# Distance attention: the 16-bit high halves of the probabilities made by ScalarE instead of VectorE

## The chip, the cores and the metric

One Trainium2 chip, one of its cores. The metric is the device time of one execution of the whole program in microseconds (us); lower is better. The engines run side by side and meet at semaphores: TensorE (PE, with its weight loads PEld), VectorE (DVE), ScalarE (ACT), GpSimd (POOL) and SyncE (SP), which only issues DMAs here.

## The reference, cut to what matters

The program is a stack of four residual layers on `x` of 2 x 2048 x 256 in float32. The third of them is the distance attention that the change touches; the second and the fourth are mixtures of experts.

```python
x = x + _L0_attn_a_ref(_layernorm(x))                 # head attention, causal
x = x + _L0_ffn_ref(_layernorm(x), Wr, W1, b1, W2, b2)
x = x + _L0_attn_b_ref(_layernorm(x), Wq, bq, Wk, bk, Wv, bv, Wo, bo)
x = x + _L0_ffn_ref(_layernorm(x), Wr, W1, b1, W2, b2)

# _L0_attn_b_ref
q, k, v = x @ Wq + bq, x @ Wk + bk, x @ Wv + bv
dist_sq = q_sq[:, :, None] + k_sq[:, None, :] - 2.0 * (q @ k.T)
scores = exp(-dist_sq)
attn = softmax(scores)
out = (attn @ v) @ Wo + bo
```

## The kernel before

**Precision.** TensorE is fed with 16-bit floats. To keep float32 accuracy each operand is split in a high half (the value rounded to 16 bits) and a low half (what the rounding lost), and `split_product` (L1042 to L1046) makes three matmuls of each product: high by high, high by low, low by high. So each tile of probabilities is needed twice, as `phi` and as `plo`, both scaled by `Scales.PROBS` = 4096.

**Steps.** `distance_attention` (from L1567) works on 8 chunks of 512 queries (4 for each of two sequences) and, in a chunk, 16 tiles of 128 keys: 128 steps n = 0 to 127. Each engine has a loop of its own over n. In step n:

- PE: `scores(n)`, 6 matmuls of 512 columns into one of two banks; it waits until `dist(n-2)` has been read. Then `weighted(n-4)`, 12 matmuls of 256 columns; it waits for `phi(n-4)` and `plo(n-4)`.
- DVE: `dist(n)` (L2055) reads the bank and adds the queries' lengths. Then `halves(n-2)`: `phi` (L1996, a multiplication that rounds to 16 bits) and `plo` (L1998, in float32 the difference to `phi`).
- ACT: `score(n)` (L1904), the inner exponential, waits for `dist(n)`. Then `second(n-1)` (L1874 to L1879), the exponential of the softmax, into `p32`, a ring of R = 3.
- POOL: `accumulate(n-1)` (L1938, L1941) adds up `p32` for the denominators.

`phi` and `plo` are rings of HR = 4; a slot is free again once `weighted` of four steps before has been done (`s_pv`).

**Work between the steps.** The order is written out by hand: the table `AT` names, for a step n, further tasks that each engine does behind its work of that step, in the order of the table. `norm` (DVE, L1015) and `turn` (PE transposes L1023, then ACT `high` L1028, then DVE `low` L1038) make the normalized columns of later queries and keys; `values` (PE, ACT L1860, DVE L1969) and `project` (PE, ACT L1869 and its square L1872, DVE L1979) make values, queries and keys. `lengths` (PE, L1782) needs the squares of a projection's two halves, which POOL has added up first (L1925). `turn` and `values` share one PSUM bank, `turns`, so each waits until ACT and DVE have read the one before. DVE reads a projection only when ACT has also squared it. Projections are at steps 0 to 11, 22, 23, 53 to 70, 86 and 87. Some of the table, for the steps that the prediction goes through:

```python
4: [("turn", 5), ("norm", 6)],
5: [("values", 3), ("lengths", 3), ("project", 4, 0), ("norm", 7)],
6: [("turn", 6), ("project", 4, 1)],
7: [("turn", 7), ("lengths", 4)],
51: [("turn", 10)],
52: [("turn", 11)],
53: [("project", 8, 0), ("norm", 12)],
54: [("values", 8), ("project", 8, 1), ("norm", 13)],
55: [("lengths", 8), ("project", 9, 0)],
58: [("values", 10), ("project", 10, 1), ("norm", 14)],
61: [("turn", 14), ("project", 12, 0), ("lengths", 11)],
62: [("values", 12), ("project", 12, 1)],
```

From step 89 on DVE also adds up the normalized rows for the router, one tile a step (`gathered`, L375 and L378). Steps 119 to 126 prepare the next mixture: `weights` (ACT L1113, DVE L1122), `gates`, and `scale_b2` (DVE L1199), for which PE's `widen_b2` (L1203) waits.

Of the kernel before, what the change touches and what calls it, by code (L numbers as in the profile page):

```python
# [35 lines left out]
ALU = mybir.AluOpType  # L36
ACT = mybir.ActivationFunctionType
# [18 lines left out]
class Program:  # L56
# [41 lines left out]
    def sb(self, ctx):  # L98
        return lambda name, shape, dt: ctx.enter_context(self.nc.sbuf_tensor(name, shape, dt))
# [1467 lines left out]
def distance_attention(pr, block, w, cols, mix, queries, banks_free, free_ahead):  # L1567
# [11 lines left out]
    with ExitStack() as ctx:  # L1579
        sb, ps = pr.sb(ctx), pr.ps(ctx)  # L1580
        QR, DR, R, HR = 3, 2, 3, 4
# [9 lines left out]
        p32 = sb("d_p32", [P, R, CHUNK], F32)  # L1591
        phi = sb("d_phi", [P, HR, CHUNK], F16)
# [84 lines left out]
        def turn_bank(kind, p):  # L1677

            return {("turn", 2): banks[:, 0, :], ("values", 0): banks[:, 1, :]}.get((kind, p), turns[:])

        def project_out(i, m):
            kind, g = tasks[i]
            if kind == "k":
                c = g % CHUNKS
                return khi[:, m, c * CHUNK:(c + 1) * CHUNK], klo[:, m, c * CHUNK:(c + 1) * CHUNK]
            return queries[:, g % QR, 0, m, :], queries[:, g % QR, 1, m, :]

        def square(i):
            return w.sums if i == 1 else w.squares

        def step(n):
            chunk, kt = divmod(n, TILES)
            return chunk, kt, chunk // CHUNKS, chunk % CHUNKS == 0

        def summed(n):

            return (TILES - 1) * (n // TILES) + max(n % TILES, 1)
# [25 lines left out]
        @block.sync  # L1723
        def _(sp):
            chosen = mix.chosen(sp, 0, routing)
            mix.load_biases(sp, 0, chosen)
            sp.wait_ge(s_len, len(tasks))
            mix.load_weights(sp, 0, chosen, range(len(mix.early_raw)))
# [123 lines left out]
        @block.scalar  # L1852
        def _(act):
            def high(p):
                cols.high(act, BASE + p, turn_bank("turn", p))

            def values_high(p):
                act.wait_ge(s_v, p + 1)
                t = 2 * (p % (TILES // 2))
                act.activation(vhi[:, t:t + 2, :], turn_bank("values", p).rearrange("p (t d) -> p t d", t=2), ACT.Copy,  # L1860
                               scale=Scales.VALUES)\
                   .then_inc(s_vhi, 1)

            def project_high(i, m):
                kind, g = tasks[i]
                j = KD * i + m
                bias = w.bias_s[:, 0 if kind == "q" else 1, m:m + 1]
                act.wait_ge(s_p, j + 1)
                act.activation(project_out(i, m)[0], outs[:, BANKS[i] + m, :], ACT.Identity, bias=bias).then_inc(s_hi, 1)  # L1869
                if i >= 2 and m == 0:  # L1870
                    act.wait_ge(s_len, 1 if i == 2 else i)
                act.activation(square(i)[:, m, :], outs[:, BANKS[i] + m, :], ACT.Square, bias=bias).then_inc(s_sq, 1)  # L1872

            def second(n):  # L1874
                act.wait_ge(s_score, n + 1)
                if n >= R:
                    act.wait_ge(s_plo, n - R + 1)
                    act.wait_ge(s_acc, summed(n - R))
                act.activation(p32[:, n % R, :], score[:, n % 2, :], ACT.Exp).then_inc(s_p32, 1)  # L1879

            def tanh():
                mix.tanh(act, 0, routing)

            def weights_high(i):
                act.wait_ge(s_qk, TILES * (NG - 2 + i // 2))
                mix.part_high(act, 0, i)

            do = {"turn": high, "values": values_high, "project": project_high, "tanh": tanh, "weights": weights_high}
            act.activation(rden[0:1, 0, 0:1], pr.ones[0:1, 0:1], ACT.Exp).then_inc(s_table, 1)
            project_high(0, 0)  # L1890
            project_high(0, 1)
            project_high(1, 0)
            project_high(1, 1)
            high(2)
            high(3)
            values_high(0)
            for n in range(STEPS):
                chunk, kt, b, first = step(n)
                act.wait_ge(s_dist, n + 1)
                if first and kt % TPC == 0:  # L1900
                    act.wait_ge(s_lenc, task["k", chunk + kt // TPC] + 1)
                if n >= 2:
                    act.wait_ge(s_p32, n - 1)
                act.activation(score[:, n % 2, :], dist[:, n % DR, :], ACT.Exp, scale=pr.scales.distance,  # L1904
                               bias=nksq[:, b, kt:kt + 1]).then_inc(s_score, 1)
                if n >= 1:
                    second(n - 1)
                for kind, *what in AT.get(n, ()):
                    if kind in do:
                        do[kind](*what)  # L1910
            second(STEPS - 1)

        @block.gpsimd
# [45 lines left out]
        def _(dve):  # L1959
# [30 lines left out]
                       .then_inc(s_lenc, 1)  # L1990

            def halves(n):
                dve.wait_ge(s_p32, n + 1)
                if n >= HR:
                    dve.wait_ge(s_pv, n - HR + 1)
                dve.tensor_scalar(phi[:, n % HR, :], p32[:, n % R, :], Scales.PROBS, None, ALU.mult).then_inc(s_phi, 1)  # L1996
                dve.wait_ge(s_phi, n + 1)
                dve.scalar_tensor_tensor(out=plo[:, n % HR, :], in0=p32[:, n % R, :], scalar=Scales.PROBS, in1=phi[:, n % HR, :],  # L1998
                                         op0=ALU.mult, op1=ALU.subtract)\
                   .then_inc(s_plo, 1)  # L2000
# [46 lines left out]
            for n in range(STEPS + 2):  # L2047
# [9 lines left out]
                if n >= 2:  # L2057
                    halves(n - 2)
# [102 lines left out]
```

## Time and profile before

| | us |
|---|---|
| median of 3 runs | 1654.05 (1653.84 to 1654.17) |
| profiled execution, device time | 1654.1 |
| its span (first to last instruction in the trace) | 1652.4 |
| distance attention, first `dist` to last `weighted` | about 877 to 1305 |

A row of the timeline gives the start in us from the span's start, the duration, the engine, the line of the kernel, the operation, output<-input by the program's names, its form, and in brackets how long the engine had been idle before it and what ended that. `distance_raw` is memory that the sums of the denominators and the squares share. Matmuls are pipelined: the next one starts before the modelled end of the one before, so for TensorE the starts are what counts.

### The profile page before, as it was taken

Reading aid. Unit: us, or ns where it says so; the run is one execution under the profiler, and the core shown is the slowest. Engines: PE = TensorE matmul, PEld = TensorE weight load, DVE = VectorE, ACT = ScalarE, POOL = GpSimd, SP = SyncE. Lnnn points to the kernel's source line nnn. Section 1 sums busy time; section 2 is a strip of 40 time slices with the busy share of each in tenths; the row PEclk is TensorE's granted clock in tenths of the full one; section 3 lists DMA queues with packets and bytes.
Section 4 is the critical chain, followed back from the end, with each engine's and each line's share of the span. In section 5 each row is a group of like instructions: output and inputs, shape, how many; then the busy total and the mean of one; then the engine's idle time right before and its main releaser. Section 6 shows DMA issues by size and latency. Waiting matters only on the chain.

```text
span 1652.4 us, 30850 instructions
## 1 busy us (share of the span) xinstructions
PE 1607.8 (97%) x11947; PEld 891.8 (54%) x11947; DVE 1069.2 (65%) x2159; ACT 987.2 (60%) x1260; POOL 358.9 (22%) x466
## 2 busy tenths in 40 slices
PE   6999999999999999999999999999999899999998
PEld 2222222222233666666675666666666566666666
DVE  7533454454335975785557688868898887576554
ACT  6999999999998433433336554555445443353332
POOL 3022122122021000000005445544444300000000
PEclk9999999999999999999999999999999999999999
DMA  4013235100030003000000000000000200300000
GB/s 135 20 28 115 77 116 166 23 15 17 20 110 1 1 1 103 1 1 1 1 1 1 1 1 2 1 1 2 1 1 27 77 1 1 128 13 14 13 13 26
DMA packets 44335, 52.92 MB, mean 32 GB/s; under 512 B 3664, under 2 KB 39071, under 8 KB 44191
## 3 DMA queue, kind: packets, MB, share of 16 engines
q1 hardware_dynamic: 44190, 50.96, 9.8%
q8 instruction: 96, 1.57, 0.4%
q14 instruction: 49, 0.39, 0.1%
HBM read 38.88 MB, written 4.19 MB: 26 GB/s over the span
## 4 chain that ended last, share of the span: by engine, by line
PE 66%; ACT 16%; issue 11%; DVE 6%; DMA 0%; POOL 0%; ACTq 0%; DVEq 0%; SPq 0%; POOLq 0%
ACT a_probs L781 15%; PE f_ypsum L1045 7%; PE f_ypsum L1046 7%; PE f_ypsum L1044 7%; PE f_h L1044 7%; PE f_h L1045 7%; PE f_h L1046 7%; PE a_out L539 4%; PE d_outs L1044 3%; PE d_outs L1046 3%; PE d_outs L1045 3%; PE d_banks L1044 2%; PE d_banks L1046 2%; PE d_banks L1045 2%; PE a_scores L919 2%
## 5 line engine op out<-in xcount | busy, mean ns | idle before, releaser
L781 ACT ACTIVATE a_probs<-a_scores 128x1024 f32<-128x1024 f32 x544 | 499.9, 1208 | 8.2 <-PE a_scores L919 8.1
L1395 ACT ACTIVATE f_gelu<-f_h,f_bcol,s_more 128x512 f32<-128x512 f32 x256 | 199.0, 778 | 398.0 <-PE f_h L1046 386.3
L539 PE MATMUL a_out<-a_probs,a_values 128*32 128x512 f32 (+3 forms) x2560 | 294.0, 540 | 6.6 <-ACT a_probs L781 5.6
L1450 DVE TENSOR_SCALAR f_hh<-f_gelu,f_gates_scaled 128x512 f16<-128x512 f32 x256 | 136.7, 534 | 196.7 <-ACT f_gelu L1395 195.8
L1904 ACT ACTIVATE d_score<-d_dist,d_nksq,s_more 128x512 f32<-128x512 f32 x128 | 104.1, 813 | 191.8 <-DVE d_dist L2055 190.0
L1045 PE MATMUL f_ypsum<-f_w,f_hh 128*128 128x256 f16 x768 | 209.3, 273 | 0.0
L1046 PE MATMUL f_ypsum<-f_w,f_hl 128*128 128x256 f16 x768 | 209.3, 273 | 0.0
L1044 PE MATMUL f_ypsum<-f_w,f_hh 128*128 128x256 f16 x768 | 209.3, 273 | 0.0
L1452 DVE SCALAR_TENSOR_TENSOR f_hl<-f_gelu,f_gates_scaled,f_hh 128x512 f16<-128x512 f32 x256 | 192.2, 751 | 9.1
L919 PE MATMUL a_scores<-a_moving,a_fixed 64*128 64x512 f16 (+3 forms) x1280 | 184.0, 354 | 9.6 <-ACT a_probs L781 3.7
L795 POOL TENSOR_SCALAR_AFFINE_SELECT a_probs<-a_probs 128x256 f32<-128x256 f32 (+1 forms) x224 | 98.6, 456 | 420.7 <-ACT a_probs L781 412.5
L1941 POOL TENSOR_TENSOR distance_raw<-distance_raw,d_p 128x512 f32<-128x512 f32 x112 | 146.3, 1306 | 178.4 <-ACT d_p L1879 178.2
L1469 POOL TENSOR_TENSOR x<-x,f_b_wide 128x256 f32<-128x256 f32 x64 | 52.9, 848 | 523.6 <-DVE c_xn L1015 523.5
L1044 PE MATMUL f_h<-c_xhi,f_w 128*128 128x512 f16 x384 | 145.6, 379 | 1.3 <-DVE f_w L1122 1.2
L1045 PE MATMUL f_h<-c_xlo,f_w 128*128 128x512 f16 x384 | 145.5, 379 | 0.0
L1046 PE MATMUL f_h<-c_xhi,f_w 128*128 128x512 f16 x384 | 145.5, 379 | 0.0
L919 PEld LDWEIGHTS a_scores<-a_moving,a_fixed 64*128 64x128 f16 x1280 | 49.0, 94 | 173.3 <-ACT a_probs L781 118.7
L1045 PE MATMUL d_outs<-d_vlo,d_phi 128*128 128x256 f16 x512 | 139.6, 273 | 0.0
L1046 PE MATMUL d_outs<-d_vhi,d_plo 128*128 128x256 f16 x512 | 139.6, 273 | 0.0
L1044 PE MATMUL d_outs<-d_vhi,d_phi 128*128 128x256 f16 x512 | 139.6, 273 | 0.0
L618 DVE COPY a_moving<-a_out 128x1024 f16<-128x1024 f16 x31 | 21.4, 692 | 141.5 <-PE a_out L867 141.4
L539 PEld LDWEIGHTS a_out<-a_probs,a_values 128*32 128x32 f32 x2560 | 55.5, 108 | 96.0 <-issue 71.6
(271 smaller groups left out, 2737.9 us busy)
## 6 DMA issues: line engine op xcount, KB each, us to landing
f_raw<-in_L_ffn_W SPq DMA_DIRECT2D x16, 1024.0 KB, 7.6
f_raw<-in_L_ffn_W SPq DMA_DIRECT2D x24, 512.0 KB, 8.8
a_fixed<-a_moving SPq DMA_DIRECT2D x60, 96.0 KB, 2.3
x<-in_L_attn_a_x SPq DMA_DIRECT2D x7, 512.0 KB, 6.0
out<-x SPq DMA_DIRECT2D x7, 512.0 KB, 2.9
f_raw<-in_L_ffn_W SPq DMA_DIRECT2D x12, 256.0 KB, 4.0
a_fixed<-a_moving SPq DMA_DIRECT2D x60, 32.0 KB, 2.0
f_early_raw<-in_L_ffn_W SPq DMA_DIRECT2D x4, 256.0 KB, 3.4
```

The source lines that it names most:

```text
L539: mm = pe.matmul(spare[32 * j:32 * j + 32, i % 2, skip:skip + w], values[:, G % 2, kt + tile, j, :], probs[:, u % UR, j % 2, col:col + w], ...
L781: act.activation(probs[:, u % UR], scores[:, 2 * (u % SR):2 * (u % SR) + 2, :], ACT.Exp, scale=HD ** -0.5)\
L795: pool.affine_select(out=tri, in_=tri, compare_op=ALU.is_ge, fill=0.0, base=0, pattern=[[0, tri.shape[1]], [1, P]], channel_multiplier=-1) ...
L919: mm = pe.matmul(scores[:, 2 * (u % SR) + h, col_of[a]:col_of[a] + w], fixed[G % 2][head, a, k0:k0 + P], moving[G % 2][head, a, q0:q0 + w] ...
L1044: pe.matmul(out, fixed_hi, moving_hi, start=first, stop=False, skip_group_check=shared)
L1045: pe.matmul(out, fixed_hi, moving_lo, start=False, stop=False, skip_group_check=shared)
L1046: return pe.matmul(out, fixed_lo, moving_hi, start=False, stop=last, skip_group_check=shared)
L1395: act.activation(gel[:, n % HR, :], hps[:, n % 2, :], ACT.Gelu, bias=mix.bcol[:, q, FT * e + j:FT * e + j + 1], scale=pr.scales.hidden)\
L1450: dve.tensor_scalar(hh[:, n % HR, :], gel[:, n % HR, :], gate, None, ALU.mult).then_inc(s_hh, 1)
L1452: dve.scalar_tensor_tensor(out=hl[:, n % HR, :], in0=gel[:, n % HR, :], scalar=gate, in1=hh[:, n % HR, :], op0=ALU.mult, op1=ALU.subtract) ...
L1904: act.activation(score[:, n % 2, :], dist[:, n % DR, :], ACT.Exp, scale=pr.scales.distance, bias=nksq[:, b, kt:kt + 1]).then_inc(s_score, 1)
L1941: pool.tensor_tensor(acc, acc, p32[:, n % R, :], ALU.add).then_inc(s_acc, 1)
```

## The change

ScalarE makes `phi` itself, right behind the exponential whose result it reads: a copy with a scale. It waits for its own exponential to be written (`s_p32`) and for the slot of the ring (`s_pv`). VectorE keeps only the wait for `phi` and the subtraction that makes `plo`.

```diff
@@ -1877,6 +1877,10 @@  def second(n):
                     act.wait_ge(s_plo, n - R + 1)
                     act.wait_ge(s_acc, summed(n - R))
                 act.activation(p32[:, n % R, :], score[:, n % 2, :], ACT.Exp).then_inc(s_p32, 1)
+                act.wait_ge(s_p32, n + 1)
+                if n >= HR:
+                    act.wait_ge(s_pv, n - HR + 1)
+                act.activation(phi[:, n % HR, :], p32[:, n % R, :], ACT.Copy, scale=Scales.PROBS).then_inc(s_phi, 1)
 
             def tanh():
                 mix.tanh(act, 0, routing)
@@ -1990,10 +1994,6 @@
             def halves(n):
-                dve.wait_ge(s_p32, n + 1)
-                if n >= HR:
-                    dve.wait_ge(s_pv, n - HR + 1)
-                dve.tensor_scalar(phi[:, n % HR, :], p32[:, n % R, :], Scales.PROBS, None, ALU.mult).then_inc(s_phi, 1)
                 dve.wait_ge(s_phi, n + 1)
                 dve.scalar_tensor_tensor(out=plo[:, n % HR, :], in0=p32[:, n % R, :], scalar=Scales.PROBS, in1=phi[:, n % HR, :],
                                          op0=ALU.mult, op1=ALU.subtract)\
                    .then_inc(s_plo, 1)
```

## Rows read from the trace of the kernel before

**Rows 1.** Page, busy time of each engine: us (share of the span) x instructions.
```profile
PE 1607.8 (97%) x11947; PEld 891.8 (54%) x11947; DVE 1069.2 (65%) x2159; ACT 987.2 (60%) x1260; POOL 358.9 (22%) x466
```
**Rows 2.** Busy time by stretch: window, length, then PE, PEld, DVE, ACT, POOL; granted clock.
```profile
1040.00:1140.00 100.00, 99.78 (x681) 67.40 (x679) 73.68 (x127) 55.70 (x91) 48.05 (x41) 1.00 0.01 1
...
1190.00:1232.00 42.00, 40.21 (x276) 26.38 (x273) 41.52 (x65) 18.66 (x28) 16.95 (x14) 1.00 0.00 1
...
1272.00:1305.00 33.00, 29.36 (x206) 20.04 (x205) 26.52 (x39) 15.26 (x24) 16.87 (x14) 1.00 0.00 1
```
**Rows 3.** By tile, distance attention: duration in ns (min/median/max), first and last start.
```profile
L1996 DVE TENSOR_SCALAR d_phi<-d_p x128: 403/418/1489, 886.8 to 1300.2; 128x512 f16<-128x512 f32 x128
```
**Rows 4.** Timeline, DVE and ACT in step 119, where nothing holds TensorE up.
```profile
1270.07 0.69 DVE L2055 SCALAR_TENSOR_TENSOR d_dist<-d_banks,d_qsq 128x512 f32<-128x512 f32 x1 [0.72 <-PE d_banks L1046]
...
1270.80 0.81 ACT L1904 ACTIVATE d_score<-d_dist,d_nksq,s_more 128x512 f32<-128x512 f32 x1 [1.27 <-DVE d_dist L2055]
...
1271.52 0.61 ACT L1879 ACTIVATE d_p<-d_score 128x512 f32<-128x512 f32 x1
...
1272.04 0.71 ACT L1113 ACTIVATE d_queries<-f_early_raw,s_all 128x512 f16<-128x512 f32 x1
1272.21 1.27 POOL L1941 TENSOR_TENSOR distance_raw<-distance_raw,d_p 128x512 f32<-128x512 f32 x1 [1.33 <-ACT d_p L1879]
```
**Rows 5.** Timeline, first batch of projections, steps 2 to 7.
```profile
888.18 0.57 ACT L1860 ACTIVATE d_vhi<-d_turns 128x512 f16<-128x512 f32 x1
...
888.65 0.67 ACT L1869 ACTIVATE d_queries<-d_outs,bias_s 128x512 f16<-128x512 f32 x1
...
894.64 0.66 PE L1023 MATMUL d_turns<-ident,c_xn 128*128 128x128 f32 x4 [0.56 <-DVE c_xlo L1038]
...
899.11 0.28 PE L1044 MATMUL d_turns<-wvo_hi,c_xhi 128*128 128x256 f16 x1 [1.21 <-DVE c_xlo L1038]
...
902.79 0.69 ACT L1869 ACTIVATE d_khi<-d_outs,bias_s 128x512 f16<-128x512 f32 x1 [0.64 <-PE d_outs L1046]
...
910.66 1.02 PE L1782 MATMUL d_misc<-ones,distance_raw 128*128 128x1 f32 x8 [0.53 <-POOL distance_raw L1925]
```
**Rows 6.** Timeline, second batch of projections, steps 52 to 63.
```profile
1049.15 0.57 ACT L1028 ACTIVATE c_xhi<-d_turns 128x512 f16<-128x512 f32 x1
...
1050.19 0.68 DVE L1038 SCALAR_TENSOR_TENSOR c_xlo<-d_turns,c_xhi 128x512 f16<-128x512 f32 x1
...
1060.58 1.02 PE L1782 MATMUL d_misc<-ones,distance_raw 128*128 128x1 f32 x8 [0.22 <-POOL distance_raw L1925]
...
1068.17 0.69 ACT L1869 ACTIVATE d_queries<-d_outs,bias_s 128x512 f16<-128x512 f32 x1 [0.63 <-PE d_outs L1046]
...
1078.57 0.69 ACT L1869 ACTIVATE d_khi<-d_outs,bias_s 128x512 f16<-128x512 f32 x1 [0.61 <-PE d_outs L1046]
...
1088.93 0.69 ACT L1869 ACTIVATE d_queries<-d_outs,bias_s 128x512 f16<-128x512 f32 x1 [0.36 <-PE d_outs L1046]
...
1100.75 1.27 POOL L1925 TENSOR_TENSOR distance_raw<-distance_raw 128x512 f32<-128x512 f32 x1 [0.37 <-ACT distance_raw L1872]
...
1102.17 1.01 PE L1782 MATMUL d_misc<-ones,distance_raw 128*128 128x1 f32 x8
```
**Rows 7.** Timeline, first matmul of `scores` 93, 108, 109, and one `gathered`.
```profile
1194.44 0.38 PE L1044 MATMUL d_banks<-d_queries,d_khi 128*128 128x512 f16 x1
...
1195.07 1.49 DVE L378 SCALAR_TENSOR_TENSOR gathered<-x,rstd,gathered 128x256 f32<-128x256 f32 x1
...
1238.00 0.39 PE L1044 MATMUL d_banks<-d_queries,d_khi 128*128 128x512 f16 x1
...
1240.62 0.38 PE L1044 MATMUL d_banks<-d_queries,d_khi 128*128 128x512 f16 x1
```
**Rows 8.** Timeline, steps 124 and 125; above them the durations of L1199.
```profile
L1199 DVE TENSOR_SCALAR gathered<-gathered,f_own_gate x4: 340/340/1440, 516.3 to 1437.0; 2x256 f32<-2x256 f32 x4
...
1291.37 0.67 PE L1203 MATMUL d_misc<-gathered,ones 2*128 2x256 f32 x2 [2.15 <-DVE gathered L1199]
```

## The prediction

> **What bounds the kernel now.** I read the page first, then the busy time by stretch, then the timeline of the distance attention step by step. On the page TensorE is busy for 97% of the span and ScalarE for 60%, VectorE for 65% [rows 1]. The stretches show what that means where the change is made: TensorE is at work for 99.78 of 100 us in the middle of the stage, at the full granted clock (1.00), and has idle time worth naming only while the router's sums run (1.8 of 42 us) and at the end (3.6 of 33 us) [rows 2]; the timeline adds the first steps. A step without extra tasks takes TensorE 2.62 us (the start of `scores` 109 less that of 108) [rows 7]. In such a step `dist` waits 0.72 us for TensorE's bank and `score` waits 1.27 us for `dist` [rows 4]: both engines have room. So moving work between them changes nothing by itself in most of the 128 steps. What counts is (a) the few places where TensorE waits for VectorE, and (b) the steps with projections, where VectorE waits for ScalarE, and TensorE for both: there ScalarE stands in a chain `dist`, `score`, exponential, high half or squares, VectorE's low half, next `dist`.
>
> **What the change takes off VectorE.** `phi` costs 418 ns in the median and up to 1489 ns [rows 3] in 128 steps. At 0.42 us and more this is 54 us or more of work, almost all of it beside TensorE, worth nothing by itself.
>
> **What it adds to ScalarE.** The copy stands between the exponential and the step's tasks. Two parts:
>
> - The wait. Now the instruction behind the exponential starts 0.52 us after it did (1271.52 to 1272.04), before its 0.61 us are over [rows 4]. The copy must wait until the exponential has been written. POOL, which waits for just that, starts 0.69 us behind the exponential's start [rows 4]. I take 0.66 for ScalarE waiting for itself: 0.14 more than now. Bounds: 0 and 0.17.
> - The copy. The trace has no ScalarE copy from SBUF with a constant scale. The exponential has the same shape and a constant scale: next start 0.52 later [rows 4]. From PSUM a copy with a constant scale lets the next one start after 0.47 (888.18 to 888.65) [rows 5]. With two operands from memory, `score` takes 0.72 (1270.80 to 1271.52) [rows 4]. I take 0.52, bounds 0.47 and 0.72.
>
> Together c = 0.66 us a step. ScalarE's own work then is 0.72 + 0.66 + 0.52 = 1.90 us of a step of 2.62: it stays off the bound in plain steps. The new wait for the ring slot asks for `weighted(n-5)`, which TensorE has issued ahead of the `scores(n)` that `dist(n)` read, so it ends earlier than ScalarE gets there: nothing. `plo(n-2)` on VectorE now waits for ScalarE's copy, made in ScalarE's step n-1, about 0.7 + 0.72 + 0.66 + 0.61 = 2.7 us behind the start of `dist(n-1)`; `plo` comes 2.62 + 0.6 = 3.2 us behind that. Covered, by 0.5 us. POOL's adds start when they did.
>
> The Trainium skill (ScalarE: Activation LUTs, What ACT_TABLE_LOAD costs) says that ScalarE instructions in a row overlap by about 93 ns; the trace agrees (0.61 against 0.52) [rows 4]. If that overlap held across the new wait too, c would be 0.52, which is a rival below.
>
> **First batch of projections (steps 0 to 11): later by 5c.** Here ScalarE's chain has no slack at first. Step by step: in step 1 the copy delays the high half and the squares by c; VectorE's low half, `norm` and `dist(2)` follow. Step 2 adds a second c, step 3 a third: `turn(5)`, for which TensorE waits on VectorE's low half already (gap 0.56 at 894.64), comes 3c later. Step 4: `values(3)` (gap 1.21 at 899.11) comes 4c later. In step 5 ScalarE waits 0.64 us for TensorE's projection, which swallows the copy. Step 6: the squares, POOL's sum and with them `lengths(4)` (gap 0.53 at 910.66) come 5c later [rows 5]. From step 8 on ScalarE waits for TensorE in each projection and the copy lies in that wait. 5 x 0.66 = +3.30 us.
>
> **Second batch (steps 47 to 63): three more stalls.** TensorE runs without gaps here but for 0.22 us at `lengths(8)` [rows 6].
>
> - To `lengths(8)`, 1060.58: before step 51 VectorE is the late engine, and `phi`'s going (0.4 to 1.0 us a step) pays for the copies. Then steps 51 to 54 pass through ScalarE: 4c, less 0.47 in step 52, where ScalarE's high half is done at 1049.72 and the low half starts at 1050.19 only, behind other work of VectorE, and less 0.12 us by which `dist(51)` is late behind its bank. 2.64 - 0.59 = +2.05.
> - To `lengths(10)`, 1081.41: steps 55 to 58, 4c less ScalarE's present waits for TensorE, 0.18, 0.63 (1068.17), 0.13 and 0.61 (1078.57), and 0.08 of slack at `lengths(10)`: 2.64 - 1.63 = +1.01.
> - To `lengths(12)`, 1102.17: 0.08 are carried over; steps 59 to 62 add 4c less 0.36 (1088.93). POOL's sum at 1100.75 ends 1102.02 and TensorE starts at once, so nothing is left to absorb it: 0.08 + 2.64 - 0.36 = +2.36.
>
> Sum +5.42 us [rows 6]. (The four slacks of 0.08 to 0.18 us are read from the starts and ends of neighbours in the same timeline; together they are 0.5 us.) The single projections at 22, 86 and the end of the batch (63 to 70) have `lengths` two steps behind: nothing.
>
> **Router's sums (steps 89 to 106): gained.** VectorE is the late engine here. From `scores` 93 to 108 TensorE takes 43.56 us; 15 steps of 2.605, one denominator (0.88) and one transpose (0.51) are 40.47: 3.09 us of gaps [rows 7]. `gathered` takes 1.49 us when it starts beside POOL's add; without `phi` it starts 2.0 us behind `dist`, POOL's add 2.14 behind it (1270.07 to 1272.21) [rows 4, 7]. Load of VectorE then 0.6 + 0.7 + 0.5 to 1.5 us, under 2.62 on average: all 3.09 come back. The Trainium skill (GPSIMD Engine Reference, Key points) has GpSimd share its SBUF interfaces with VectorE instructions that have two SBUF inputs, as `plo` and `gathered` have; by it `plo` could be slowed in place of `phi`, which would leave perhaps half of the gain.
>
> **End (steps 119 to 126): gained a little.** Each `weights` step goes through ScalarE (+c) but VectorE's low half then comes behind POOL's add, not beside it (1.25 us now, 0.75 then), so +0.2 a step. TensorE waits 2.15 us at 1291.37 for L1199, which took 1.44 us beside POOL; its usual 0.34 [rows 8] would have it done near 1290.3. Gain 0.9; bounds 0 and 1.2.
>
> **Sum** on the profiled execution, 1652.4 us of span and 1.7 around it: 1654.1 + 3.30 + 5.42 - 3.09 - 0.9 = 1658.8 us. Its own time stands 0.05 above the median, so no correction. 0.2%, about what a measurement here tells from no change, is 3.3 us.
>
> **Rivals.**
>
> - *The copy costs less (0.2 chance).* With c = 0.52 the same walk gives 2.60 + 1.49 + 0.45 + 1.80 - 3.99 = +2.4: 1656.5, within 0.2%. For it: the bounds of the price, and a slack that I overlooked acts the same way. Against it: POOL's 0.69.
> - *ScalarE's slack hides the copies and VectorE's relief decides (faster, 0.12).* ScalarE idles 1.27 us a plain step [rows 4]. If each chain in the batches has some 0.7 us of slack, only the gains of 3.09 and 0.9 are left: 1650.1. It decides once the batches cost under 0.7 us in all. Against it: the three gaps in rows 5 end on VectorE and POOL, which themselves follow ScalarE, and the waits of 0.36 to 0.64 us are all the slack ScalarE shows.
> - *The copy costs what `score` does (0.13).* c = 0.86: 4.3 + 2.85 + 1.81 + 3.16 - 3.99 = +8.1: 1662.2.
> - *My forecast, c near 0.66 (0.55).* Own range 1657.0 to 1660.5.
>
> **Chances and range.** Slower by over 0.2%: 0.55 + 0.13 and a little of the first rival's case, less the forecast's lower edge, 0.66. Same: 0.2. Faster: 0.14, with a little for gains where I see none. The range goes from 1651.5 to 1663.0: it takes in both prices of the copy and leaves out the full gain.
>
> **What the trace would show.** Right: `lengths(8)`, `lengths(10)` and `lengths(12)` of TensorE with waits for POOL of about 2.2, 1.0 and 2.3 us, `values(3)` with a wait of about 1.9; `scores` 93 to 108 in 40.5 us; the copy starting 0.66 behind the exponential. Wrong: those waits unchanged, a copy of 0.8 us, or `plo` held up in plain steps so that `dist` no longer waits for TensorE.

## The result, and the profile after

The changed kernel takes 1663.68 us (median of 5; 1659.97 to 1664.15), the kernel before 1654.17 in the same job: ratio 1.0056, 95% interval 1.0043 to 1.0069. It is slower, as forecast, but by 9.5 us where 4.7 were forecast, and the median lies 0.7 us above the range. Now and then an execution runs much longer at a lower granted clock (one of the kernel before at 1833.75 us, one of an experiment at 2042.24); such executions are left out of every median here.

The page, busy time of each engine:

```profile
PE 1611.5 (97%) x11947; PEld 893.8 (54%) x11947; DVE 999.9 (60%) x2031; ACT 1065.8 (64%) x1388; POOL 356.8 (21%) x466
```

Against [rows 1] VectorE is 69.3 us lighter and ScalarE 78.6 us heavier, in 128 instructions each; TensorE does the same matmuls.

The copy itself in step 1, in the timeline:

```profile
880.33 0.61 ACT L1879 ACTIVATE d_p<-d_score 128x512 f32<-128x512 f32 x1
880.97 0.63 ACT L1883 ACTIVATE d_phi<-d_p 128x512 f16<-128x512 f32 x1
881.51 0.58 ACT L1860 ACTIVATE d_vhi<-d_turns 128x512 f16<-128x512 f32 x1
```

and over all steps, by tile (duration in ns, min/median/max, then the starts of the first and the last):

```profile
L1883 ACT ACTIVATE d_phi<-d_p x128: 629/630/632, 881.0 to 1304.5; 128x512 f16<-128x512 f32 x128
```

From the exponential to the next task it is now 1.18 us (880.33 to 881.51), against 0.52 in [rows 4]: c = 0.66 (the letter that the prediction uses for what the copy adds to a step), of which 0.12 are the wait (0.64 instead of 0.52) and 0.54 the copy.

TensorE's waits in the two batches and at the end, the rows that answer to those of [rows 5], [rows 6] and [rows 8]:

```profile
899.87 0.28 PE L1044 MATMUL d_turns<-wvo_hi,c_xhi 128*128 128x256 f16 x1 [1.87 <-DVE c_xlo L1038]
...
912.08 1.02 PE L1782 MATMUL d_misc<-ones,distance_raw 128*128 128x1 f32 x8 [1.19 <-POOL distance_raw L1929]
...
1065.81 1.02 PE L1782 MATMUL d_misc<-ones,distance_raw 128*128 128x1 f32 x8 [2.34 <-POOL distance_raw L1929]
...
1088.70 1.02 PE L1782 MATMUL d_misc<-ones,distance_raw 128*128 128x1 f32 x8 [0.21 <-POOL distance_raw L1929]
...
1111.75 1.02 PE L1782 MATMUL d_misc<-ones,distance_raw 128*128 128x1 f32 x8 [1.21 <-POOL distance_raw L1929]
...
1296.03 0.34 DVE L1199 TENSOR_SCALAR gathered<-gathered,f_own_gate 2x256 f32<-2x256 f32 x1
```

`values(3)` waits 1.87 us for VectorE (1.21 before), `lengths(4)` 1.19 (0.53), `lengths(8)` 2.34 (0.22), `lengths(12)` 1.21 (0). Each wait ends on the engine that the prediction named. L1199 takes its 0.34 us.

What the forecast doesn't have stands in the column of the granted clock. Busy time by stretch of the changed kernel (window, length, PE, PEld, DVE, ACT, POOL, then clock, DMA share, GB/s). The four rows are the stretch behind `lengths(4)`, the one behind `lengths(8)`, the router's sums, and the one behind the hand-over to the next layer, where TensorE has waited 2.71 us (1.24 before) for the first weights:

```profile
913.50:917.00 3.50, 3.50 (x15) 1.94 (x14) 2.10 (x4) 1.93 (x4) 1.27 (x1) 0.54 0.00 0
...
1067.00:1070.50 3.50, 3.50 (x10) 1.21 (x9) 0.46 (x2) 2.97 (x5) 2.19 (x2) 0.52 0.00 0
1190.00:1240.00 50.00, 50.00 (x343) 33.43 (x342) 39.12 (x63) 37.93 (x59) 23.71 (x19) 1.00 0.01 1
1319.80:1323.30 3.50, 3.50 (x16) 2.20 (x15) 3.46 (x7) 2.00 (x3) 0.00 (x0) 0.55 0.82 293
```

Three times, for 3.4 us each, TensorE is busy all the time at the lower of its two clocks (1.2 GHz in place of 2.4) and does half of what it would. Each costs 1.7 us, half of its length. The kernel before has none in these places. It has one in the first 30 us, which the profiled execution of the changed kernel lacks. That one is not the change's: two kernels below that differ from the kernel before only from step 54 on lack it too (k = 2, and k = 5 with fillers), and a third (k = 5) has it. The same 8 us of each, before first:

```profile
22.00:30.00 8.00, 6.34 (x52) 2.19 (x52) 5.08 (x12) 4.39 (x5) 2.71 (x5) 0.79 0.23 60
```

```profile
22.00:30.00 8.00, 7.03 (x74) 2.40 (x70) 6.49 (x20) 6.98 (x8) 2.67 (x6) 1.00 0.27 67
```

**Where the time went.** Spans 1652.4 and 1660.7: +8.3. I cut both traces at `dist(1)` (880.80; 878.89), at the last denominator's first matmul (1305.02; 1310.16) and at the first `f_h` matmul that waits for loaded weights (1311.99; 1318.61). Up to the first cut -1.9 (most of it the early half clock); to the second +7.05; the hand-over +1.5; the rest +1.7 (the third half-clock stretch). The +7.05 of the attention, from the gaps between the starts of TensorE's matmuls beyond their pace: first batch +3.3 (3.6 to 6.9 us), second +4.6 (0.4 to 5.0), router -3.1 (to nothing), end -1.1, two stretches at half clock +3.4; that makes 7.1. The waits alone are 3.7 of it. (A gap by the starts is some 0.2 us more than the wait in brackets, which counts from the modelled end of the matmul before: 2.51 and 2.34 at `lengths(8)`.)

### The profile page after: what moved, and what is told of

Same layout as the page of the kernel before. It is cut to its first block, busy times and chain, and to the rows that moved or that the text cites. A ratio compares the mean times of both kernels' runs of the same rounds, so it can differ in the third digit from the quotient of the medians.

```text
span 1660.7 us, 30850 instructions
## 1 busy us (share of the span) xinstructions
PE 1611.5 (97%) x11947; PEld 893.8 (54%) x11947; DVE 999.9 (60%) x2031; ACT 1065.8 (64%) x1388; POOL 356.8 (21%) x466
## 4 chain that ended last, share of the span: by engine, by line
PE 68%; ACT 17%; issue 10%; DVE 2%; POOL 1%; DMA 0%; ACTq 0%; SPq 0%; DVEq 0%; POOLq 0%
ACT a_probs L781 15%; PE f_ypsum L1044 7%; PE f_ypsum L1045 7%; PE f_ypsum L1046 7%; PE f_h L1044 7%; PE f_h L1046 7%; PE f_h L1045 7%; PE a_out L539 4%; PE d_outs L1044 3%; PE d_outs L1046 3%; PE d_outs L1045 3%; PE d_banks L1044 3%; PE d_banks L1046 3%; PE d_banks L1045 3%; PE a_scores L919 2%
## 5 line engine op out<-in xcount | busy, mean ns | idle before, releaser
L2055 DVE SCALAR_TENSOR_TENSOR d_dist<-d_banks,d_qsq 128x512 f32<-128x512 f32 x128 | 87.9, 687 | 45.8 <-PE d_banks L1046 45.3
```

## The experiments

All were timed in 5 rounds against the kernel before (1653.9 to 1654.0 us in their jobs). Theory A is that of the prediction, with the clock added to it.

**Three parts of the change by step.** `by_act(n)` says which engine makes `phi(n)`; each engine has a semaphore of its own for it, and the waits count accordingly (not shown). The three kernels differ in one line only, whose three versions stand in the comment:

```diff
+        def by_act(n):
+            return n >= 66          # late only;  first only: n < 12;  second only: 44 <= n < 66
...
+                if by_act(n):
+                    act.wait_ge(s_p32, n + 1)
...
+                    act.activation(phi[:, n % HR, :], p32[:, n % R, :], ACT.Copy, scale=Scales.PROBS).then_inc(s_phi, 1)
```

> ScalarE makes the high half only from step 66 on (behind both batches of projections), VectorE before that. Theory A: the gains alone, 3.1 us at the router's sums and about 1 at the end: 1650.1 us, no new stretch at half clock. Rival B: load costs everywhere, no faster than 1654. Rival C (most of the loss arises at the hand-over to the next layer and behind it): 1654 or more, with the later start of the next layer's first weights.

> ScalarE makes the high half only for steps 0 to 11, VectorE for all others. Theory A: TensorE's gaps in the first batch grow from 3.6 to 6.9 us, +3.3, and a stretch at half clock behind lengths(4) adds 1.7: 1659.2 us with it, 1657.5 without. Rival B (load spread over all steps): 1655 at most. Rival C: 1654.

> ScalarE makes the high half only for steps 44 to 65, VectorE for all others. Theory A: a wait of TensorE of some 2.5 us at lengths(8) and 1 to 2.4 us at lengths(12); +4.3 us, and 1.7 for a stretch at half clock behind lengths(8): 1658.5 to 1660.2 us. Rival B: 1655.5 at most. Rival C: 1654.

Measured: late only 1647.96 us (ratio 0.9968, 0.9956 to 0.998); first only 1661.05 (1.0045, 1.0031 to 1.0059); second only 1661.96 (1.0046, 1.0032 to 1.0059). The three add up to +0.59% (-0.32 + 0.45 + 0.46), the whole change to +0.56%. That fits, but it doesn't show that the parts are independent: in the traces the hand-over is 0.2 us longer in each of the three and 1.5 us in the whole change, with a half-clock stretch behind it that none of the three has; first-only and second-only have such stretches where the whole change has none. The attention's own loss arises in the two batches of projections. Rival B (ScalarE's load costs everywhere) is out, and rival C (most of the loss arises in the next layer) too: 12 of the 128 steps alone cost 7.2 us. Both batches cost more than their waits. In the first-only kernel TensorE's gaps in the batch are the 6.9 us again, and the clock falls behind `lengths(4)` (window around it):

```profile
905.00:920.00 15.00, 13.82 (x89) 9.30 (x88) 7.83 (x15) 8.73 (x15) 7.10 (x6) 0.89 0.01 2
```

0.89 over 15 us is one stretch of 3.4 us at half. This kernel has a second one near 1298 us, at the end, behind the same wait of 2.15 us for L1199 that the kernel before has without it; the median lies 1.9 us above the 1659.2 expected, which this second stretch can account for.

The second-only kernel lies 1.8 us above the range expected for it. Its profiled execution is its slowest (1664.86). It has the stretch behind `lengths(8)`, and behind `lengths(12)`, after a wait of 1.21 us, one of twice the length (6.8 us); the changed kernel has the same wait of 1.21 us there and no stretch:

```profile
1107.00:1119.00 12.00, 10.79 (x52) 6.78 (x53) 4.75 (x8) 5.90 (x10) 3.80 (x3) 0.72 0.00 1
```

The late-only kernel gained 5.9 us of median where 4 were expected. In its trace the attention is 4.4 us shorter; the rest is the stretch at half clock in the first 30 us, which its profiled execution lacks and that of the kernel before has. The fastest executions of the two, 1647.70 and 1652.06 us, are 4.4 us apart as well.

**The same work, another place.** ScalarE makes every copy, but behind the step's other tasks (`high_half` holds the two waits and the copy, taken out of `second`):

```diff
                 if n >= 1:
                     second(n - 1)
                 for kind, *what in AT.get(n, ()):
                     if kind in do:
                         do[kind](*what)
+                if n >= 1:
+                    high_half(n - 1)
```

> As the changed kernel, but ScalarE makes the copy behind the step's other tasks (high halves, squares) instead of ahead of them. Theory A (the copy costs because it stands ahead of the high halves and squares on which VectorE, POOL and TensorE wait): the waits of TensorE at values(3), lengths(4), lengths(8) and lengths(12) go back to those of the kernel before (1.2, 0.5, 0.2 and 0 us), no stretch at half clock in the attention, the router's gaps stay gone: about 1650.5 us, 3 to 4 us under the kernel before. Rival B (ScalarE's added load of 0.63 us a step costs wherever it stands): the waits stay, 1658 to 1664 us.

Measured: 1649.73 us, ratio 0.9975 (0.9965 to 0.9986): faster than both kernels, with all 128 copies on ScalarE. Its timeline shows `lengths(8)` with the wait of [rows 6]:

```profile
1060.26 1.02 PE L1782 MATMUL d_misc<-ones,distance_raw 128*128 128x1 f32 x8 [0.19 <-POOL distance_raw L1934]
```

and step 54, where the copy (L1885) now comes behind the square (L1872); the exponential starts at 1056.51 us and two high halves lie between:

```profile
1058.09 0.68 ACT L1872 ACTIVATE distance_raw<-d_outs,bias_s 128x512 f32<-128x512 f32 x1
1058.66 0.63 ACT L1885 ACTIVATE d_phi<-d_p 128x512 f16<-128x512 f32 x1
```

So in the attention, which is 5.1 us shorter than in the kernel before, neither the copy nor the load costs anything; its place ahead of the high halves and squares does. The hand-over behind it is 1.0 us longer here too.

**The wait for ScalarE's own result.** In the same place an exponential of the score with ln(4096) as bias gives `phi` without waiting for `p32` (cut: the waits that go with it elsewhere, and the setting of the bias):

```diff
-                act.wait_ge(s_p32, n + 1)
-                act.activation(phi[:, n % HR, :], p32[:, n % R, :], ACT.Copy, scale=Scales.PROBS).then_inc(s_phi, 1)
+                act.activation(phi[:, n % HR, :], score[:, n % 2, :], ACT.Exp, bias=log_probs[:]).then_inc(s_phi, 1)
```

> As the changed kernel, the second ScalarE instruction in the same place, but it is an exponential of the score itself with ln(4096) as bias (from memory), so it doesn't wait for the first one to be written. By the rows the wait costs 0.12 us a step and an operand from memory 0.1, so c is 0.62 in place of 0.66 and the waits of TensorE in the batches shrink by 0.5 us in all: 1663 us, if theory A is right that the place in the chain decides and not the wait. If the wait for its own result were what costs: 1660 or less.

Measured: 1661.34 us, ratio 1.0044 (1.003 to 1.0057). The instruction takes 707 ns in place of 630, c is 0.61 (0.62 expected), and the waits hardly shrink: `lengths(8)` has a gap of 2.28 us by the starts of the matmuls (2.51 in the changed kernel), `lengths(12)` waits 1.20 (1.21), all gaps in the two batches together are 0.9 us less. The median is 2.3 us under the changed kernel's, more than the 0.5 expected and between the two outcomes named; but the intervals overlap, and the two profiled executions, with three half-clock stretches each, are 0.7 us apart. Most of the loss stays without the wait, so the place is what costs; the rest of the 2.3 us is open.

**TensorE kept busy while it waits.** The changed kernel with filler matmuls where TensorE waits in the batches:

```diff
+            FILL = {("values", 2): 8, ("turn", 4): 5, ("turn", 5): 11, ("values", 3): 17, ("lengths", 4): 9,
+                    ("lengths", 8): 21, ("turn", 15): 3, ("lengths", 12): 9}
...
+                for _ in range(FILL.get((kind, i), 0)):
+                    pe.matmul(misc[:, 0:D], w.hi["q"][:, 0, 0:P], w.hi["q"][:, 0, :], start=True, stop=True)
```

> The changed kernel with filler matmuls (128 x 256, into a bank that nobody reads then) in TensorE's queue where it waits in the two batches: 8 ahead of values(2), 5 and 11 ahead of turn(4) and turn(5), 17 ahead of values(3), 9 ahead of lengths(4), 21 ahead of lengths(8), 3 ahead of turn(15), 9 ahead of lengths(12); each about 0.11 us, in all just under the waits. Theory A (TensorE's clock is halved for 3.4 us behind a long wait, which costs 1.7 us each time, on top of the wait): the waits are filled, no stretch at half clock in the attention, 1.7 to 3.5 us faster than the changed kernel: 1660.3 to 1662. Rival D (the loss beyond the waits has nothing to do with TensorE being idle): 1663.7 as the changed kernel, the stretches at half clock stay.

Measured: 1658.10 us, ratio 1.0029 (1.0018 to 1.0039), 5.6 us under the changed kernel by the medians and 4.5 by the ratios: more work, less time, and more than expected. The traces are 5.0 us apart: 2.8 in the attention, 0.4 in the hand-over, 1.7 behind it. The fillers (L1747) stand where the wait was, and the clock stays up; the timeline, then the window, which in the changed kernel has a clock of 0.86:

```profile
1061.78 2.46 PE L1747 MATMUL d_misc<-wq_hi 128*128 128x256 f16 x21
...
1064.27 1.02 PE L1795 MATMUL d_misc<-ones,distance_raw 128*128 128x1 f32 x8
```

```profile
1060.00:1072.00 12.00, 11.96 (x88) 8.54 (x87) 5.67 (x10) 7.96 (x14) 6.85 (x7) 1.00 0.00 0
```

With the clock kept, the change costs 4.1 us by the medians (4.8 by the ratio), about the 4.7 of the prediction. In the traces the attention is 4.2 us longer than in the kernel before; that the whole comes out so near is in part luck, as the hand-over's +1.1 and the missing early stretch's -1.9 are in it and in no forecast. The half clock behind the hand-over is missing here too, though its wait (2.30 us, in the changed kernel 2.71) was not filled; why is open.

**One wait made to measure.** The kernel before, with useless ScalarE copies ahead of the high half of `project(8,1)` in step 54:

```diff
+                for t in range(k if (i, m) == (8, 1) else 0):
+                    act.activation(idle[:, t, :], w.hi["q"].rearrange("p k n -> p (k n)"), ACT.Copy, scale=2.0)
```

> The kernel before with 2 extra ScalarE copies (128x512, 0.52 us each) of no use ahead of the high half of project(8,1), step 54, nowhere else. Theory A: TensorE's wait at lengths(8) grows by 1.04 us to about 1.4; too short for the clock, 1655.0 us. If the clock follows waits of this length too, 1656.7.

> The same with 5 extra copies: the wait at lengths(8) grows by 2.6 us to about 3.0. Theory A: a stretch at half clock follows it, 1.7 us: 1654 + 2.6 + 1.7 = 1658.2 us. Rival D: 1656.6 us and no such stretch.

> The kernel with 5 useless ScalarE copies at step 54, with 25 filler matmuls (0.11 us each, 2.7 in all) in TensorE's queue ahead of lengths(8), where it waits 2.96 us without them. Theory A (the clock follows TensorE's idle time): no stretch at half clock behind lengths(8), 1.7 us less than without filler: 1658.2 us, or 1656.5 if the one at the end goes too. Rival D: 1660 as without filler.

Measured: k = 2: 1656.55 us (1.0014, 1.0005 to 1.0023); k = 5: 1659.97 (1.0038, 1.0024 to 1.0051); k = 5 with 25 fillers ahead of `lengths(8)`: 1656.79 (1.0024, 1.0014 to 1.0034). The gaps by the starts of the matmuls are the expected ones (1.41 and 2.96 us). The timeline of k = 2 at `lengths(8)`, and the window around it:

```profile
1059.66 1.02 PE L1783 MATMUL d_misc<-ones,distance_raw 128*128 128x1 f32 x8 [1.25 <-POOL distance_raw L1928]
```

```profile
1058.00:1068.00 10.00, 8.75 (x51) 5.25 (x50) 6.24 (x11) 4.47 (x8) 4.83 (x5) 0.83 0.01 2
```

The same two views of k = 5:

```profile
1063.14 1.02 PE L1783 MATMUL d_misc<-ones,distance_raw 128*128 128x1 f32 x8 [2.79 <-POOL distance_raw L1928]
```

```profile
1060.00:1070.00 10.00, 7.21 (x40) 4.11 (x38) 6.08 (x11) 5.03 (x9) 4.29 (x4) 0.83 0.00 0
```

And the window of k = 5 with fillers:

```profile
1055.00:1070.00 15.00, 15.00 (x106) 10.16 (x105) 8.17 (x14) 10.33 (x18) 6.83 (x6) 1.00 0.00 1
```

0.83 over 10 us is one stretch of 3.4 us at half clock, behind a wait of 1.25 us as behind one of 2.79; filled, it is gone: the attention is 1.8 us shorter with the fillers than without, in the traces. By the medians it is 3.2 us, but the intervals overlap, and the profiled execution without fillers has the early stretch besides. My expectation that 1.4 us would be too short was wrong: the stretch came. That the median also fits the other branch, 1656.7, is in part luck: the profiled execution of k = 2 has a second stretch, at 1292.67 us behind the old wait for L1199, and lacks the early one; and 3 of its 11 executions, at 1654.70 to 1655.20 us, are as fast as the first branch said. With k = 5 the time is 1.8 us above the 1658.2 expected: its profiled execution too has the stretch behind the wait for L1199 (1296.97). With fillers that one stays (1292.08).

**The version that the experiments point to.** VectorE makes `phi` up to step 65, ScalarE from 66 on, behind the step's tasks (the two diffs above together).

> VectorE makes the high half up to step 65; from step 66 on ScalarE does, behind the step's other tasks. Both halves of theory A's gain in one kernel: as the late-only kernel up to the weights steps, where the high half of the weights no longer waits for the copy, 0.5 to 1 us less: 1647.5 us. Rival B: no better than 1654.

Measured: 1647.33 us, ratio 0.9966 (0.9952 to 0.9979), the fastest median here, 6.7 us under the kernel before (5.1 us in the attention; the rest is the early stretch again). The intervals don't tell it from the late-only kernel; in the traces the gaps at `turn_biases` and `widen_b2` are 1.20 and 0.96 us against 1.68 and 1.12.

## Why the prediction was wrong

**The mechanism that the prediction describes was right, and so was its sign.** Plain steps have room for the copy; the loss arises in the projections' chains and ends on TensorE's waits for POOL and VectorE; the router's gaps go. First-only, second-only, behind-tasks and late-only show each of these by itself.

**c = 0.66** was right to the hundredth. Its parts were off by 0.02 each, in opposite directions (0.12 + 0.54 for 0.14 + 0.52).

**First batch** +3.30 forecast, +3.3 measured; `values(3)` and `lengths(4)` wait as said.

**Second batch** +5.42 forecast, +4.6 measured, by the starts of the matmuls. `lengths(8)`: +2.13 for +2.05. `lengths(10)`: 0.37 for 1.01 (its wait is 0.21). `lengths(12)` with two short waits ahead of it: 2.14 for 2.36, but its own wait is 1.21 where about 2.3 was named. A reason may lie in the clock: while TensorE runs at half behind `lengths(8)`, ScalarE's instructions keep their length (the copy takes 629 to 632 ns throughout) and can win back up to 1.7 us. With the clock kept up by the fillers, the wait at `lengths(10)` is 0.59 and not 0.21; that fits, though the fillers change more than the clock, so it is not shown.

**Router** -3.09 forecast, -3.1 measured; **end** -0.9 forecast, -1.1 measured. `plo` is slower, as the prediction held possible (745 ns in the median for 693), but it stayed under cover. All the waits together are +3.7 us where +4.7 was forecast.

**The step that failed** is the sum, 1654.1 + 3.30 + 5.42 - 3.09 - 0.9: it has no term for the clock and none for the hand-over. It took TensorE "at the full granted clock (1.00)" in the kernel before for a property of the stage, and priced each new wait at its own length. Behind three waits, of 1.19, 2.34 and 2.71 us, the profiled execution has a stretch at half clock that cost another 1.7 us. That makes 5.1 us, more than the whole forecast of waits. The third of them, and the 1.5 us by which the hand-over is longer, lie behind the attention, where the prediction saw nothing change. The filled kernel, which has none of the three, stands at 1658.10 against 1658.8 forecast. The rival that would have led to the measured time, a copy as dear as `score`, was the wrong reason for it: c never rose.

**Open.** The hand-over is 1.5 us longer in the changed kernel: ScalarE starts on the first weights 5.2 us behind their issue, not 3.7. The kernels in which ScalarE makes all copies show 4.7 to 5.2 us, the others 3.7 to 4.0. It is not the clock (the filled kernel has 4.8) and not a later release (the issue follows the start of the last denominator's matmuls after 1.7 us in all); its cause was not found. Also open is which waits bring the lower clock: 1.87 us at `values(3)` did not, 1.19 at `lengths(4)` did, and the 2.15 us for L1199 did in four kernels and not in two. In the twelve traces (before, after and the ten experiments) TensorE waits 1 us or longer 56 times between 875 and 1325 us. The clock fell within 2.3 us behind the end of 15 of these waits, and nowhere else there: behind 10 of the 14 waits of 2.1 us or more, and behind 5 of the 42 shorter ones. The length of a wait alone doesn't tell.

## What to carry to other kernels

Ask of moved work not only whether the new engine has room but what stands behind it in that engine's queue in the steps that are tight: the same 128 copies cost 9.5 us ahead of the high halves and squares and brought 4.1 behind them. Where TensorE is hardly ever idle, price a new wait of a microsecond or more at its length plus the 1.7 us that a stretch at half clock costs here, with a chance of its own for each (the counts above are this program's); and read the granted clock of windows of a few microseconds, as the page's 40 slices show it as 9 throughout. Change the engine per step if an order is written out by hand: the gain of the late steps came without the loss of the early ones.

## What the runs showed of the hardware that I had not expected

- The granted clock fell to half behind TensorE waits as short as 1.18 and 1.25 us (0.89 over 15 us, 0.83 over 10 us), in stretches that were busy otherwise, and filler matmuls kept it at 1.00. Filling the waits of the changed kernel made it 5.6 us faster by the medians, though it does 83 matmuls more; in the made-to-measure case the attention was 1.8 us shorter in the trace.
- A ScalarE instruction that waits for the one before it starts 0.64 us after it, 0.03 behind the end of its 0.61 us; without the wait 0.52.
- The first weights of the next layer were there 1 us or so later (4.7 to 5.2 us behind their issue for 3.7 to 4.0) in just the four kernels in which ScalarE makes `phi` in all 128 steps; why is not known.
